# Sums of query tiles 1 to 3 moved ahead among the statistics and scale links in VectorE's order

## What is computed

```python
q1 = fake_quant(layernorm(x), x1_scale, x1_zp)      # 8 bits
q2 = fake_quant(ctx, x2_scale, x2_zp)               # 8 bits
x  = x + q1 @ q2                                    # stage 1
xf = layernorm(x)
combine = top-2 softmax weights of xf @ W_router.T  # 8 experts
h   = einsum('nd,erd->ner', xf, A_stack) * combine  # rank 16 per expert
x   = x + xf @ W_base.T + b_base + 2 * einsum('ner,eor->no', h, B_stack)
```

## Time and profile before

| what | value |
|---|---|
| median of 3 runs | 193.7 us (193.64 to 194.05) |
| the profiled execution's own time | 193.71 us |
| its span, first to last instruction | 191.9 us |
| around the span | 1.8 us |
| TensorE busy | 165.2 us (86% of the span) |
| VectorE busy | 140.3 us (73%) |
| ScalarE busy | 83.7 us (44%) |
| GpSimd busy | 29.2 us (15%) |
| mean granted TensorE clock | 0.982 |

### The profile page before, as it was taken

One profiled execution on the slowest core, in us unless ns is written; L12 is line 12 of the kernel. 1 busy time (PEld: TensorE's weight loads), 2 busy tenths in 40 slices (PEclk: granted clock), 3 DMA queues, 4 the chain that ended last, 5 costly groups with the idle time before them and its releaser, 6 DMA issues.

```text
span 191.9 us, 2629 instructions
## 1 busy us (share of the span) xinstructions
PE 165.2 (86%) x946; PEld 87.7 (46%) x946; DVE 140.3 (73%) x413; ACT 83.7 (44%) x109; POOL 29.2 (15%) x20
## 2 busy tenths in 40 slices
PE   6857793859967497788699999999999999999993
PEld 3322341325534134436266566466466466466541
DVE  6897898997966499999794793793893893841821
ACT  3466797096879896651522322322322322320000
POOL 8910000049533606000000000000000000000000
PEclk9999999699999889999999999999999999999999
DMA  5999999999400000000020020020020010110121
GB/s 114 400 418 407 411 408 406 410 360 324 178 0 7 0 0 0 0 0 3 0 109 0 3 111 0 0 113 0 22 87 3 40 69 0 61 54 0 80 84 55
DMA packets 6780, 22.74 MB, mean 118 GB/s; under 512 B 880, under 2 KB 1136, under 8 KB 6768
## 3 DMA queue, kind: packets, MB, share of 16 engines
q1 hardware_dynamic: 6624, 22.58, 30.6%
q10 hardware_dynamic: 144, 0.00, 0.0%
HBM read 18.38 MB, written 4.19 MB: 118 GB/s over the span
## 4 chain that ended last, share of the span: by engine, by line
PE 49%; DVE 22%; issue 14%; DMA 6%; SPq 3%; ACT 3%; POOL 1%; DVEq 0%; POOLq 0%; ACTq 0%
PE ps L779 36%; DMA xs<-in_x 6%; DVE w_lo L558 6%; PE ps L769 5%; PE ps L748 3%; DVE xs L490 2%; SPq L185 2%; ACT junk L289 2%; PE ps L760 1%; PE ps L762 1%; PE ps L761 1%; DVE diag L511 1%; POOL xs L228 1%; DVE rsq L430 1%; DVE rsq L432 1%
## 5 line engine op out<-in xcount | busy, mean ns | idle before, releaser
L739 PE MATMUL ps<-a,a_t 128*128 128x512 f16 x128 | 34.9, 409 | 9.4 <-issue 5.8
L779 PE MATMUL ps<-w_hi,yt_hi 128*128 128x512 f16 x128 | 39.5, 380 | 3.0 <-DVE w_lo L558 3.0
L779 PE MATMUL ps<-w_hi,yt_lo 128*128 128x512 f16 x128 | 39.4, 379 | 0.0
L779 PE MATMUL ps<-w_lo,yt_hi 128*128 128x512 f16 x128 | 39.4, 379 | 0.0
L228 POOL TENSOR_TENSOR xs<-xs,corr 128x1024 f32<-128x1024 f32 x8 | 19.7, 2482 | 45.7 <-DVE q_bias L461 30.6
L739 PEld LDWEIGHTS ps<-a,a_t 128*128 128x128 f16 x128 | 12.4, 104 | 26.0 <-issue 10.3
L249 ACT ACTIVATE a<-stage,prm,inv_s 128x1024 uint8<-128x1024 f32 x16 | 19.6, 1238 | 9.9 <-DMA stage<-in_ctx_kv 9.6
L779 PEld LDWEIGHTS ps<-w_hi,yt_lo 128*128 128x128 f16 x128 | 12.5, 98 | 15.1
L779 PEld LDWEIGHTS ps<-w_lo,yt_hi 128*128 128x128 f16 x128 | 12.5, 98 | 14.8
L313 ACT ACTIVATE y<-xs,y_bias,y_scale 128x1024 f32<-128x1024 f32 x8 | 9.9, 1236 | 19.4 <-DVE y_bias L506 19.4
L779 PEld LDWEIGHTS ps<-w_hi,yt_hi 128*128 128x128 f16 x128 | 11.5, 98 | 14.8 <-DVE w_lo L558 3.7
(11 more groups left out here) (122 smaller groups left out, 255.2 us busy)
## 6 DMA issues: line engine op xcount, KB each, us to landing
stage<-in_ctx_kv SPq DMA_DIRECT2D x16, 512.0 KB, 13.6
stage<-in_w_t SPq DMA_DIRECT2D x8, 512.0 KB, 10.5
xs<-in_x SPq DMA_DIRECT2D x7, 512.0 KB, 13.8
out_dram<-xs SPq DMA_DIRECT2D x7, 512.0 KB, 2.7
ar_raw<-in_ar_t SPq DMA_DIRECT2D x1, 544.0 KB, 15.4
xs<-in_x SPq DMA_DIRECT2D x2, 256.0 KB, 3.8
b_raw<-in_b_t SPq DMA_DIRECT2D x1, 512.0 KB, 6.0
bias_sb<-in_bias SPq DMA_DIRECT2D x1, 512.0 KB, 6.7
```

What stands on the lines that cost most here:

```text
L739: last = nc.tensor.matmul(ps[:, s1_bank(t) + h, :], a1_t[:, t % 4, k, :], a2[:, n, h * H:(h + 1) * H], start=k == 0, stop=k == K - 1)
L779: ins = nc.tensor.matmul(ps[:, OUT_BANK[p] + h, :], part, rhs[:, k, h * H:(h + 1) * H], start=k == 0 and part is hi and rhs is w_hi, stop= ...
```

## The change

Only VectorE's order changes. No instruction is added or taken away, and all other engines keep their lists. Both pairs' `prepare_pair` are written out as their parts, so that the sums of tiles 1, 2 and 3 can stand between them.

```diff
             quantise_x(2)
             quantise_x(3)
             sum_x1(0)
-            prepare_pair(4)
+            statistics_x(4)
+            sum_x1(1)
+            statistics_x(5)
+            scale_x(4, 2)
             quantise_x(4)
-            sum_x1(1)
+            sum_x1(2)
             quantise_x(5)
-            prepare_pair(6)
-            sum_x1(2)
+            statistics_x(6)
+            statistics_x(7)
             sum_x1(3)
+            scale_x(6, 2)
             scale_y((0, 1))
             sum_x1(4)
             peaks_ar()
```

## The result

The changed kernel takes 196.13 us in the median of 4 runs (195.71 to 197.03), the kernel before 193.67 us (193.55 to 194.05, 4 runs). The ratio is 1.0122, with a 95% interval of 1.0102 to 1.0141. The forecast was 196.1 us, with a range of 195.5 to 197.1.

What follows compares the result with a forecast made beforehand. The chain through GpSimd's first corrections, `diag` and ScalarE's peaks was taken to set the start of TensorE's busy second stage; 193.71 us (profiled execution) + 2.39 = 196.10, so 196.1 us, range 195.5 to 197.1.

Steps and rivals of the forecast that it cites:

- What bounds the kernel: Stage 1 path: end of the last links, two GpSimd corrections, `scale_y`, `sum_x1(4)`, `diag`, `scale_ar`, ScalarE's peaks.
- The term that counts: VectorE: two sums now ahead of the links of tiles 6 and 7 delay GpSimd's start by 2.39 us.
- The gaps of TensorE: Stage 1: 3.69 us gap gone; new waits about 1.5 us before tile 4's transposes, some 3 us at block 15.
- Tile 5 "some 3.5 us": TensorE, tile 5's start to L811: 14 matmuls and the transposes, some 3.5 us, arriving at about 51.4.
- The term of the clock: TensorE behind L811: low clock could make ScalarE late, 0 to +1.0 us; taken as nothing, rival's chance 0.12.
- the slack: ScalarE at `take_a1t(7)`: arrives at 62.39, transposes end at 62.3 with a low clock as long as seen, just fitting.
- TensorE's path decides (faster): Rival: second stage's start follows TensorE's work, so 1.7 us left at tile 5 comes off, 192.0 us; chance 0.04.
- the gap of 3.69 us: TensorE's idle time ahead of tile 3's product, released by the sum of tile 1; forecast to vanish.
- The earlier tile 4: TensorE: tile 4's product starts at about 36 instead of 42.19, 6 us earlier.
- `diag` escapes GpSimd: Rival: GpSimd's fifth correction gets the port after both L511 instructions; 2.19 us go away, 193.91 us; chance 0.06.

Runs made afterwards that it cites:

- the kernels with the filling matmuls: Kernels with no sum, and with two, put ahead of the links of tiles 6 and 7, plus spare-data matmuls where TensorE stands idle: 193.73 and 195.93 us.
- the last pair of kernels: Kernel before with GpSimd's corrections placed singly: old VectorE order 190.96 us; sums 1 and 2 ahead, sum 3 behind the links of tiles 6 and 7, 189.15 us.
- the kernel with one sum ahead: The changed kernel with the sum of tile 3 put back behind the links of tiles 6 and 7: 195.59 us.

## Why the prediction was right, point by point

*What bounds the kernel.* Right. GpSimd's first correction, released by L461, carries the loss, and taking away or adding one sum ahead of L461 moves it by one pitch. `split_ar` was forecast at 58.93 and L544 at 67.68; they came at 58.65 and 67.40 in an execution that was 0.34 us ahead.

*The term that counts.* 2 x 1.195 = 2.39 us was predicted. The traces give 1.19 for each sum, counted from the sum of tile 0; the medians give 2.46 for the change and 2.20 between the kernels with the filling matmuls that have none and two sums ahead.

*The gaps of TensorE.* Right in place: 1.40 us ahead of the transposes of tile 4 where 1.5 was said, 2.81 us for block 15 where some 3 was said, tile 5 at 47.4 where 47.8 was said.

*Tile 5 "some 3.5 us".* This step failed. I priced tile 5 at the full clock and placed the low clock only behind L811. It fell earlier, behind the stands of 2.81 and 1.04 us, and TensorE came to L811 at 53.8 and not at 51.4. The stand there was 2.96 us instead of 5.7. It cost nothing, because `diag` was later still.

*The term of the clock.* Taken at 0, with +1.0 as upper bound. In the profiled execution ScalarE lost nothing: the twelve matmuls took 4.19 us, the transposes of tile 7 were done at 61.5, and ScalarE came to their copy at 62.12. I said that this fits by 0.1 us; it fits by 0.6. One piece was left out: the matmul over `diag` runs at the low clock itself, 0.37 us instead of 0.27, and VectorE waits 0.56 us for it instead of 0.45, so 0.1 us did reach the path. And the reason I gave, that the slack covers a low clock as long as the one seen, is weak. I expected a stand of 5.7 us; the one kernel that has it, with one sum less ahead, runs all twelve matmuls at the low clock, in 5.28 us, and ScalarE waits 0.45 us for it. That the changed kernel escaped this is luck: its clock fell earlier, in tile 5, and the stand became shorter. One of its four runs took 197.03 us at a mean clock of 0.956, which lies where this rival put it; no profile shows that run. The chance of 0.12 was low for this.

*TensorE's path decides (faster).* Refuted. In after tile 4's transposes and products are the earlier ones that I forecast, and TensorE still stands 2.96 us for `diag`. With only the gap of 3.69 us taken away and the clock kept up, the time is 193.73 us against 193.80. The earlier tile 4 is worth something only once GpSimd's corrections are placed: 1.8 us in the last pair of kernels.

*`diag` escapes GpSimd.* It did not, and the pair took 2.59 us as before. The point that I gave, both released by `sum_x1(4)`, holds. The worth of 2.19 us that I put on an escape was too high: with `diag` freed the hold went to `scale_ar`, and 1.0 us was gained against the change (+1.45 instead of +2.46 against before). To get more the correction has to stay clear of both. In the kernel with only the sum of tile 1 ahead `diag` did escape (0.41 us for the pair), because the correction waited for `make_corr(1)`.

## What to carry to other kernels

Before an instruction is moved ahead in an in-order queue, list who waits for what it is moved past, not only who waits for the moved one: here the released engine had slack, and the one made to wait, which does little work and looks idle, was on the path. A coarse wait (all eight scales before the first correction) turns such a shift into a loss of its whole length; with the corrections placed singly the same sort of move gained. And an idle engine's longer stand can be a cost of its own when its clock falls in it: after a gap is closed, look at the next stand, not only at the sum of them.

## What the runs showed of the hardware

GpSimd's correction (two inputs and the output in SBUF, 2.35 us) holds some VectorE instructions until it ends, small ones too: 128x2 links took 2.23 and 1.54 us instead of 0.17, the second `diag` 2.43 instead of 0.25, and in `split_w` three took 5.77 us instead of 3.67. Sums that read PSUM, bn_stats, and the links of `scale_y` over one number per partition ran beside it at their usual length, 1.28, 0.69 and 0.46 us for a pair. In the other direction, with its wait taken out in the kernel before, the second correction started 0.16 us behind the start of `quantise_x(5)` and took 2.85 us. The Trainium skill, SBUF — State Buffer, section SBUF: two separate sides, calls the port pair that the two engines share an exclusive lock that whoever starts first has for its whole instruction. The traces agree in both directions: the held links end within 0.02 us of the correction's end (43.02 and 43.00, 57.69 and 57.67), and the correction that started second ran 0.5 us longer. The prediction had the rule from another page as mutual blocking, and did not ask which instruction would be the next one blocked.

TensorE's granted clock was at 0.50 to 0.52, the 1.2 GHz level, behind stands of 5.70 and 5.96 us, and in after also behind two of 2.81 and 1.04 us with four matmuls between them (ten matmuls of tile 5 in 4.45 us); behind a shorter pair, 1.62 and 1.09 us, in the kernel with one sum ahead, it stayed at 1.00. A stand of 2.81 us alone was enough once: in the kernel whose fifth correction waits for `diag` the four matmuls behind it ran at 0.50. With VectorE's old order the first two products of tile 4, behind a stand of 2.1 us, took 0.59 us in the profile before and 0.99 us in the one with GpSimd's wait taken out. How much of the scatter from run to run the clock makes is not shown, since each kernel has one profile; the sum of tile 0 lay anywhere from 24.82 to 25.64 us in them.
